# A graph-attention kernel: TensorE's signal of the weighted sums, once per two blocks in place of once per block

## The reference, cut to what matters

```python
for l in range(L):                                   # L = 2, H = 8 heads of DH = 32, D = 256
    xn = _layernorm(h, ln1_g[l], ln1_b[l])
    q, k, v = ((xn @ w[l] + b[l]).reshape(n, H, DH) for w, b in ((wq, bq), (wk, bk), (wv, bv)))
    scores = jnp.einsum('ehd,ehd->eh', q[dst], k[src]) * scale
    m = jax.ops.segment_max(scores, dst, num_segments=n)
    ex = jnp.exp(scores - m[dst])
    z = jax.ops.segment_sum(ex, dst, num_segments=n)
    agg = jax.ops.segment_sum((ex / z[dst])[:, :, None] * v[src], dst, num_segments=n)
    h = h + agg.reshape(n, TD) @ wo[l] + bo[l]
    h = h + gelu(_layernorm(h, ln2_g[l], ln2_b[l]) @ w1[l] + b1[l]) @ w2[l] + b2[l]
```

## Time and profile before

| what | value |
|---|---|
| runs shown | 3860.8, 3872.09, 3874.86 us |
| the profiled execution | 3861.7 us, its span 3859.9 us |
| mean granted TensorE clock | 0.735 of full speed |
| busy: TensorE, VectorE, ScalarE, GpSimd | 59%, 64%, 34%, 48% |
| HBM traffic over the span | 161 GB/s |

### The profile page before, as it was taken

One profiled execution on the slowest core, in us unless ns is written; L12 is line 12 of the kernel. 1 busy time (PEld: TensorE's weight loads), 2 busy tenths in 40 slices (PEclk: granted clock), 3 DMA queues, 4 the chain that ended last, 5 costly groups with the idle time before them and its releaser, 6 DMA issues. The chain is left out here.

```text
span 3859.9 us, 35539 instructions
## 1 busy us (share of the span) xinstructions
PE 2259.6 (59%) x7207; PEld 1532.8 (40%) x7208; DVE 2485.9 (64%) x3966; ACT 1328.6 (34%) x3895; POOL 1842.0 (48%) x1938
## 2 busy tenths in 40 slices
PE   5634555455555555488854555555545555587897
PEld 3422333333333333366632333333333333365676
DVE  5766777777677777534435776876777777544333
ACT  1223444444443444122213443443444434222231
POOL 4055666666666665111036666666666666121000
PEclk8866766766676676699975666676667667689899
DMA  3365766666667666321246666666666667322101
GB/s 104 110 178 166 209 208 207 208 205 215 196 207 216 201 208 192 96 68 60 81 130 181 206 208 209 205 208 209 203 208 206 202 211 214 90 60 62 47 31 34
DMA packets 246235, 623.21 MB, mean 161 GB/s; under 512 B 46779, under 2 KB 102259, under 8 KB 246074
## 3 DMA queue, kind: packets, MB, share of 16 engines
q0 software_dynamic: 149904, 471.38, 41.1%
q1 hardware_dynamic: 96170, 150.25, 11.9%
HBM read 526.62 MB, written 94.78 MB: 161 GB/s over the span
## 5 line engine op out<-in xcount | busy, mean ns | idle before, releaser
L774 POOL DMA_INDIRECT ring<-kv_table,stage_ix x1760 | 1679.7, 954 | 1005.0 <-issue 554.0
L1020 PE MATMUL bank<-qs,hot_q 128*128 x1760 | 717.1, 556 | 706.1 <-issue 424.4
L1033 PE MATMUL bank<-ring,hot_w 128*128 128x272 f32 x1760 | 689.2, 530 | 501.7 <-issue 306.1
L1940 DVE TENSOR_TENSOR ring<-ring,bank 128x1024 f32<-128x1024 f32 x440 | 532.3, 1210 | 548.4 <-issue 359.1
L1020 PEld LDWEIGHTS bank<-qs,hot_q 128*128 128x128 f32 x1760 | 464.5, 276 | 886.7 <-issue 790.3
L1033 PEld LDWEIGHTS bank<-ring,hot_w 128*128 128x128 f32 x1760 | 412.7, 254 | 757.5 <-issue 497.5
L1945 DVE TENSOR_REDUCE s<-ring 128x32 f32<-128x1024 f32 x440 | 532.6, 1210 | 4.2
L1274 ACT ACTIVATE stage_o<-bank 128x272 f32<-128x272 f32 x440 | 167.5, 385 | 525.0 <-remote 318.3
L1258 ACT ACTIVATE s<-bank 128x8 f32<-128x8 f32 x440 | 78.1, 178 | 736.5 <-remote 434.8
L1248 ACT ACTIVATE hot_q<-pos_b,row_of 128x128 f32<-128x128 bf16 x880 | 303.8, 394 | 12.6 <-DMA pos_b<-rel_d 8.9
L1957 DVE TENSOR_TENSOR bank<-ring,bank 128x512 f32<-128x512 f32 x440 | 300.6, 683 | 0.0
(11 more groups left out here) (326 smaller groups left out, 2155.7 us busy)
## 6 DMA issues: line engine op xcount, KB each, us to landing
agg_d<-stage_o SPq DMA_DIRECT2D x108, 544.0 KB
ring<-kv_table,stage_ix POOLq DMA_INDIRECT x1760
pos_b<-rel_d SPq DMA_DIRECT2D x54, 256.0 KB
kv_table<-ring SPq DMA_DIRECT2D x50, 250.0 KB
h_dram<-ring SPq DMA_DIRECT2D x15, 625.0 KB
ring<-h_dram SPq DMA_DIRECT2D x15, 625.0 KB
ring<-in_x_dram SPq DMA_DIRECT2D x10, 625.0 KB
ring<-kv_table SPq DMA_DIRECT2D x10, 625.0 KB
```

Of the source, the lines that this page charges most:

```text
L774: gps.indirect_dma_start(out=chunk[:, par * G + i, j, :], out_offset=None, in_=table, in_offset=bass.IndirectOffsetOnAxis(ap=stage_ix[:, p ...
L1020: mm = ten.matmul(q_bank(third, i)[:, 0:QC], hot_q[:, i % 4, a * P:(a + 1) * P], qs[:, bass.ds(t * QC + a * QC, QC)], start=(a == 0), stop ...
L1033: mm = ten.matmul(b_acc[i % 2][:, lo - OWN:MC], hot_w[:, i % 4, :], chunk[:, s, j, lo:ROW], start=(j == 0), stop=(j == QD // 2 - 1), skip_ ...
L1940: tt(k_, k_, q, ALU.mult).then_inc(S["q_used"], 1)
```

## The change

The signal of the sums is given with the last matmul of an odd block, and counts two. The last matmul of an even block gives none. Nobody's wait is rewritten: GpSimd (L772), ScalarE (L1263 and L1273) and VectorE (L2019) wait for the same counts as before. So whoever waits for the sums of an even block now waits for those of the odd block behind it. All block counts (220, and 4 in the last group) are even, so the totals agree. No instruction of any engine is added, taken away or moved.

```diff
@@ -1031,7 +1031,8 @@
                     for j in range(QD // 2):
                         lo = OWN if j == 0 else D
                         mm = ten.matmul(b_acc[i % 2][:, lo - OWN:MC], hot_w[:, i % 4, :], chunk[:, s, j, lo:ROW], start=(j == 0), stop=(j == QD // 2 - 1), skip_group_check=True)
-                    mm.then_inc(S["agg"], 1)
+                    if i % 2:
+                        mm.then_inc(S["agg"], 2)
```

## The result

The changed kernel takes 3931.38 us (median of 4 runs, 3919.24 to 3933.18), the kernel before in runs beside it 3870.17 us. The ratio is 1.0159, with a 95% interval from 1.0140 to 1.0178. I had forecast no change, 3872 us. The measured time lies inside the range (3790 to 3965), near the price of the slower rival (3937), but the loss is clear of the interval, and I had forecast none.

The account below looks back on a forecast made before the run. The edge stages were taken to run at GpSimd's pace plus its stops. Two outcomes, 0 and 20 us over 52 groups, gave a middle of 10 us: 3861.7 + 10 = 3871.7, say 3872 us, range 3790 to 3965.

Parts of the forecast that it names:

- the slower rival: GpSimd's steady groups: a third stop per group, 1.45 us more each, 3937 us (3900 to 3995); chance 0.37.
- the edge stages run at GpSimd's pace plus its stops: Edge stages: eight blocks of gathers, 40.1 us, plus 6.87 us of stops make a 47.0 us group.
- block 2 would wait for sums 3, one block early: GpSimd's gathers: it stops ahead of block 2 instead of block 3, after a burst of four, from 1050.0.
- form (a): Steady group, sums 5 late for block 4: bursts of two and six blocks, stops 7.47 us together, 0 more than today.
- VectorE's wait ahead of scores 7 goes: VectorE in steady groups: the wait ahead of scores 7 goes, while the long wait ahead of scores 6 stays.
- Check 3: Changed profile, ScalarE: evacuations of an even and the following odd block lie close together, with one wait ahead of the pair.
- 4.81 us after almost six: GpSimd's stop behind a burst of almost six blocks, read at 1348.82: 4.81 us, used for the steady group's stops.
- check 2: Changed profile, GpSimd: two idle times to a group, 7.5 to 7.9 us together, chains 47.0 to 47.4 us apart.
- In a layer 26 groups reuse slots, 52 in all. (a) is 0: Whole run: one steady group's price times 52; with sums 5 late for block 4, the added cost is 0.
- The reading of the lateness: TensorE signals over 7 to 8 us after GpSimd's restart wait; a stop frees them 3 to 4 us after beginning.
- sums 7 as quick and the stop as gone: Ahead of block 6, when sums 5 are late: sums 7 end 6 us after the restart, so that stop goes.
- The faster rival: GpSimd's groups: fewer signals queue, so fewer stops, 3739 to 3845 us; chance 0.25.

Follow-up runs that it names:

- E10: The changed kernel with sums 4 and 5 signalled singly, other pairs joined, against the kernel before on the prompt-signal chip: 3439.91 us, ratio 1.0009.
- E8: The kernel before, but GpSimd waits ahead of block 4 alone for sums 5, all signals single: ratio 1.0141 to the kernel before.
- E15: The kernel before, but GpSimd waits ahead of block 6 alone for sums 7, all signals single: ratio 1.0123 to the kernel before.
- E3: The kernel before with single signals kept, but GpSimd's wait and ScalarE's evacuation wait both coarsened to the odd block: 3913.19 us, ratio 1.0159.
- E12: The changed kernel with sums 4 and 5 signalled singly, other pairs joined, on a chip with late signals: ratio 1.0101 to the kernel before.
- E9: The kernel before with a plain DMA of 128 consecutive rows in each gather's place, on the prompt-signal chip: 3198.79 us against 3435.86, ratio 0.9308.
- E6: The kernel before, but gathers in groups that reuse slots bring 64 of each row's 512 values: 3861.41 us, ratio 0.9998.
- E5: The kernel before with a GpSimd pause, clearing 256 unused columns after each block's gathers: 3868.74 us, ratio 1.0030.

## Why the prediction was wrong

**Right:** that the edge stages run at GpSimd's pace plus its stops (of +71.4 us, +75.2 stand ahead of gathers); that TensorE's late signals stand behind the stops (where they are prompt, E10 has none); that block 2 would wait for sums 3, one block early; that the steady rhythm is form (a), bursts of six and two; and that VectorE's wait ahead of scores 7 goes. Check 3 came half true: one wait, and the evacuation of block 3 2.2 us behind that of block 2 (1074.22, 1076.43).

**A term mis-sized:** "4.81 us after almost six". That stop came after 23 gathers, five and three quarter blocks. After six it is 5.3 to 5.6 us. The traces of the change and of the kernel before make a small table of the usual values: a stop takes 2.6 us after two blocks, 3.1 after three, 3.8 after four, 4.4 after five, 5.4 after six. Two steady stops so cost 5.4 + 2.6 = 8.0 us in place of 7.5, and the group 47.6 (1032.13 to 1079.73) in place of 47.0, above the 47.4 of check 2. In 52 groups that would be about 30 us, but only 20 groups are of this form, and they took 0.5 us more in all. So this term is not the loss.

**The step that failed** is the one after it: "In a layer 26 groups reuse slots, 52 in all. (a) is 0". I priced one steady group and multiplied. The page of rows already had another sort of group (stops at other blocks), and I used it for durations alone. I had counted sums 5 from the chain's start, 4.2 us, and found block 4 due 1.0 us after they end. I didn't ask what delays the chain itself: at a turn of the loop it begins 3.7 to 5.6 us late, and in other groups it waits for late signals, which mostly come when GpSimd has stopped. With that the wait is no longer late by a fixed amount, but in series with the stop: 11 stops of 5.9 to 11.1 us ahead of block 4, in place of 2.66. E8 prices block 4's wait at 1.4% alone. The six groups at turns took 36.6 of the 65.5 us, where (a) had 0.

**The reading of the lateness** was too narrow as well. I had a stop let signals out "some 3 to 4 us after it begins". In the stops of 7.50 and 10.54 us the first late signal is acted on 0.1 us after GpSimd ran dry, in others up to 3.3 us after it.

**The slower rival** had a mark that came true at the six turns: a third stop, 3.8 to 4.1 us, ahead of block 0. It gave 3937 us, for a third stop in many groups at 1.45 us each. That the time came near it is luck: few groups, 5 to 8 us each at the turns. And block 6, for which I had counted sums 7 as quick and the stop as gone, was right in the changed kernel's steady groups, yet E15 shows it as a second price in the others.

**The faster rival**, that fewer signals let the queue drain sooner, has nothing for it in E3 against the change: the two lose the same.

## What to carry to other kernels

- A coarser signal costs what its latest reader then waits for. Look at what lies between the two events that are joined: between sums 2 and 3 lay only queries, and sums 3 were done long before block 2 was due (1.0005, no cost to be told), between sums 4 and 5 lay the chain (1.4% alone).
- Price a wait in the irregular groups too, one turn of every engine's loop at least, and ask whether what it waits for needs, in turn, the waiting engine to stop. The 20 steady groups showed 0.5 of the 65.5 us.
- Join signals for a reason that the trace shows. Here 220 signals fewer gave nothing back that could be told, and nothing had shown that they cost.

## What the runs showed of the hardware

On all but one of the chips that ran these kernels, TensorE's signals were acted on as much as 13.9 us late while GpSimd issued gathers (and 13.6 us in the changed kernel), and the kernel before took 3847 to 3872 us. On one chip it took 3435.86 us (13 runs, 3432.5 to 3440.1). E10's trace from there has not one stop of GpSimd. Its groups take 40.0 to 40.3 us, which is 32 gathers of 1.254 us, and VectorE waits for data instead, as its page says:

```profile
L1943 DVE TENSOR_TENSOR ring<-ring,bank 128x1024 f32<-128x1024 f32 x440 | 532.0, 1209 | 281.2 <-DMA ring<-kv_table,stage_ix 256.0
```

There the three joined pairs cost 0.1% (E10: 3439.91 us, 1.0009 [1.0000, 1.0019]), where E12, the same kernel, cost 1.0%. The kernel is 11% faster where the signals are prompt, and there this loss is all but gone. The change itself, with its pair of blocks 4 and 5, was not run there. Whether prompt signals come with the chip or with what surrounds it, no run here tells. Nor is it shown why signals are late, whether it is a stop of GpSimd that lets them out, or whether plain DMAs in the place of gathers would keep them prompt: E9 would have to run on a chip where they are late.

Two more things of note. The stops don't hang on bytes (E6), and a pause that GpSimd takes of its own accord is nearly made good by shorter stops (E5). And a signal that counts two, given by a matmul, cost nothing that these runs can tell against two single ones (E3 and the change).
